# Projections in steps of one matmul pair, packed head rows and cropped convolution taps in a four-layer image kernel

## The reference, cut to what matters

```python
def _L0_conv_ref(x, w_qkv, w_proj, b_proj):       # layer 0: attention over 1024 pixels, 8 heads of 48 channels
    qkv = jnp.einsum('oc,bchw->bohw', w_qkv, x)
    att = softmax(einsum('bhxd,bhyd->bhxy', q * scale, k))
    out = jnp.einsum('bhxy,bhyd->bhxd', att, v)
    return jnp.einsum('oc,bchw->bohw', w_proj, out) + b_proj[None, :, None, None]

def deform_block(x, ow, ob, dw, pw, pb, K):       # layer 1: for K = 3, 5, 7, each on 128 channels
    offsets = conv2d(x, ow, ob, pad=K // 2)       # dense K x K convolution, 2 K K outputs, zero padding
    out = deform_depthwise(x, offsets, dw, K, K // 2)
    return conv2d(out, pw, pb, 0)
```

## Time and profile before

| | us |
|---|---|
| median of 3 runs (lowest, highest) | 6606.05 (6603.67, 6614.61) |
| the profiled execution | 6606.96 |
| its span | 6604.7 |
| PE busy | 5836.1 (88%) |
| DVE busy | 4831.0 (73%) |
| ACT busy | 3905.2 (59%) |
| POOL busy | 782.4 (12%) |

### The profile page before, as it was taken

The page is one execution under the profiler, slowest core; times in us unless marked ns, Lnnn a source line. Parts: engine busy times, 40 slices in busy tenths (PEclk is TensorE's granted clock), DMA queues, the critical chain, the costliest instruction groups (busy, mean ns, idle before and its releaser), DMA issues. The chain is left out here.

```text
span 6604.7 us, 121718 instructions
## 1 busy us (share of the span) xinstructions
PE 5836.1 (88%) x45996; PEld 3998.1 (61%) x45996; DVE 4831.0 (73%) x10089; ACT 3905.2 (59%) x5362; POOL 782.4 (12%) x780
## 2 busy tenths in 40 slices
PE   5999999999977888988989989899889899699798
PEld 2554454454434556875568855588655688455598
DVE  6887887787765778887788877798777888344433
ACT  3766776676652557875567855578755787112142
POOL 2222211222202002001011000110100100000000
PEclk9999999999998999999989999999999899899898
DMA  4111111112104445545445545455544454211598
GB/s 145 43 56 55 40 44 55 49 39 59 44 23 134 105 105 123 124 110 118 105 117 118 119 97 129 99 126 121 117 105 108 114 124 111 96 46 41 145 234 199
DMA packets 198408, 651.46 MB, mean 99 GB/s; under 512 B 61753, under 2 KB 68849, under 8 KB 154915
## 3 DMA queue, kind: packets, MB, share of 16 engines
q1 hardware_dynamic: 177747, 604.65, 37.2%
q0 software_dynamic: 19968, 37.78, 2.2%
HBM read 538.56 MB, written 65.59 MB: 91 GB/s over the span
## 5 line engine op out<-in xcount | busy, mean ns | idle before, releaser
L2367 PE MATMUL b_p<-b_work,b_hkt 64*128 64x144 f32 (+37 forms) x27520 | 2116.5, 309 | 253.1 <-DVE b_acc L2238 149.7
L2367 PEld LDWEIGHTS b_p<-b_work,b_hkt 64*128 64x128 f32 x27520 | 1966.0, 195 | 479.9 <-DVE b_work L2313 283.2
L2313 DVE TENSOR_TENSOR b_work<-b_work 128x140 f32<-128x140 f32 (+26 forms) x5312 | 1605.5, 353 | 228.6 <-PE b_p L2367 174.7
L2208 ACT ACTIVATE b_work<-b_work,b_mcol 128x512 f32<-128x512 f32 (+6 forms) x1328 | 764.9, 647 | 1021.4 <-DVE b_work L2313 883.3
L530 ACT ACTIVATE a_ex<-a_p_t 128x1024 f32<-128x1024 f32 x512 | 523.9, 1023 | 427.3 <-PE a_p_t L466 424.5
L2212 ACT ACTIVATE b_work<-b_work,b_mrow 128x544 f32<-128x544 f32 (+6 forms) x1328 | 762.2, 645 | 0.0
L2238 DVE SCALAR_TENSOR_TENSOR b_acc<-b_p,b_dwc,b_acc 128x323 f32<-128x323 f32 (+14 forms) x1088 | 621.6, 574 | 184.5 <-PE b_p L2367 184.5
L596 DVE TENSOR_REDUCE a_nm<-a_p_x 128x1 f16<-128x1024 f32 x512 | 624.3, 1219 | 154.0 <-PE a_p_x L455 145.8
L1779 PE MATMUL b_p<-b_hp,b_ow 128*98 128x512 f32 x1568 | 721.4, 611 | 0.0
L602 DVE TENSOR_TENSOR a_el<-a_ex,a_eh 128x1024 f16<-128x1024 f32 x512 | 682.1, 1332 | 7.0 <-ACT a_eh L535 6.9
L535 ACT CAST a_eh<-a_ex 128x1024 f16<-128x1024 f32 x512 | 535.4, 1046 | 54.8 <-ACT a_ex L530 3.8
(11 more groups left out here) (224 smaller groups left out, 5811.6 us busy)
## 6 DMA issues: line engine op xcount, KB each, us to landing
b_work<-sampling_positions SPq DMA_DIRECT2D x666, 512.0 KB, 6.5
d_win<-merged_kernels SPq DMA_DIRECT2D x192, 263.0 KB, 6.7
b_xin<-x SPq DMA_DIRECT2D x24, 1024.0 KB, 9.8
a_xr<-in_x SPq DMA_DIRECT2D x12, 1536.0 KB, 10.2
x<-a_xr SPq DMA_DIRECT2D x9, 1536.0 KB, 6.1
b_xr<-x SPq DMA_DIRECT2D x13, 1024.0 KB, 18.2
x<-b_xr SPq DMA_DIRECT2D x13, 1024.0 KB, 4.6
a_xh<-in_x SPq DMA_DIRECT2D x8, 1536.0 KB, 8.6
```

The costliest lines, as they stand in the source:

```text
L2208: last = e.activation(rx[:, u, xo[c]:xo[c + 1]].rearrange("p (a b) -> p a b", a=H), pp[:, b, 1, :].rearrange("p (a b) -> p a b", a=H)[:, : ...
L2313: e.tensor_tensor(S[:, k % NS, 0:(r1 - r0) * w].rearrange("p (a b) -> p a b", b=w), rx[:, u, xo[cc]:xo[cc + 1]].rearrange("p (a b) -> p a ...
L2367: last = e.matmul(G[:, a0 - top:z0 - top, c0 - left:c1 - left], hkt[64 * s:64 * s + 64, SIDE * cr + cc, :], S[64 * s:64 * s + 64, k % NS, ...
```

## The change

In layer 0 a query or key unit takes three slots with one matmul in each, so that nearly every slot carries one fp32 matmul; `UNIT_AT` and `OUT_AT` list the slot of each part. The loop now runs from slot 26 to 89. The output projection is three matmuls per tile over 128 packed rows: the head product is made by DVE into `o` (five slots after the head's last weighing slot, where POOL's was), and POOL then copies it by DMA into `packed`, in which the 384 head rows fill three blocks of 128. The add of bias and residual comes one slot after the tile's last matmul, the last tile's at the start of `statistics`. `norm` moves to slot 86 (22 of the next image), one image earlier than its projections need it; SP's loads and stores of whole images move to other heads. In layer 1 each tap of the offset convolutions reads and writes only the rectangle that lies in the image, and the middle tap comes first. The diff, cut to its core:

```diff
-    FIRST = 14
-    BEGIN = -36
+    FIRST = 26
+    BEGIN = FIRST - STEPS
     QUERY, KEY, VALUE = range(3)
     UNIT = ([(s, 0, n) for s in (QUERY, KEY) for n in range(2)] + [(VALUE, 0, c) for c in range(4)]
             + [(s, 1, n) for s in (QUERY, KEY) for n in range(2)] + [(s, 2, n) for s in (QUERY, KEY) for n in range(2)]
             + [(VALUE, 1, c) for c in range(4)])
-    UNIT_AT = (28, 31, 34, 37, 40, 43, 45, 47, 50, 53, 56, 59, 62, 65, 78, 80, 82, 84, 86, 88)
+    UNIT_AT = ([tuple(range(m, m + 3)) for m in range(26, 38, 3)] + [(m, m + 1) for m in range(38, 46, 2)]
+               + [tuple(range(m, m + 3)) for m in range(46, 70, 3)] + [(70, 71), (72, 73), (74, 74), (82, 82)])
     UNITS = len(UNIT)
-    OUT_AT = (71, 72, 73, 75, 76, 77)
-    NORM_AT = 26
+    OUT_AT = ((75, 76, 77), (78, 78, 79), (80, 80, 81), (83, 83, 84), (85, 86, 87), (88, 88, 89))
+    NORM_AT = 86
...
+    PACK = [[(j, *piece[1:]) for j in range(G3) for piece in PIECES[j] if piece[0] == hd] for hd in range(HEADS)]
+    PACKED = [16 * sum(len(PACK[hd]) for hd in range(p, HEADS, 2)) for p in range(2)]
...
-        wp = a.sb("wp", [TP, PAIRS, C])
+        wp = a.sb("wp", [P, G3, C])
...
-        o = a.sb("o", [TP, PAIRS, N])
+        o = a.sb("o", [TP, N])
+        packed = a.sb("packed", [P, G3, N])
...
-                for g in ((0,), (1, 2))[part]:
-                    last = e.matmul(p_j[:], wqk[:, g, s, j * P:(j + 1) * P], h[:, g, n * HALF:(n + 1) * HALF], start=(g == 0), stop=(g == G3 - 1))
+                last = e.matmul(p_j[:], wqk[:, part, s, j * P:(j + 1) * P], h[:, part, n * HALF:(n + 1) * HALF], start=(part == 0), stop=(part == G3 - 1))
...
-            if part == 1:
+            if part == len(UNIT_AT[unit]) - 1:
...
-        def unit_at(m, end):
-
-            for ahead in range(0, 1 if end else 2):
-                for unit, r in enumerate(UNIT_AT):
-                    if m - r + STEPS * (1 - ahead) in (0, 1):
-                        return ahead, unit, m - r + STEPS * (1 - ahead)
-            return None
+        def parts_at(m, end):
+
+            return [(ahead, unit, part) for ahead in range(0, 1 if end else 2) for unit, ms in enumerate(UNIT_AT)
+                    for part, at_m in enumerate(ms) if m == at_m - STEPS * (1 - ahead)]
+
+        def done_at(m, end):
+
+            return [(ahead, unit) for ahead, unit, part in parts_at(m, end) if part == len(UNIT_AT[unit]) - 1]
+
+        def outs_at(m):
+
+            return [(i, part) for i, ms in enumerate(OUT_AT) for part, at_m in enumerate(ms) if m == at_m]
...
-                    if not end:
-                        e.wait_ge(s_h.sem, s_h.at(b + 1))
-                        e.sem_inc(sh["tick"], 1)
-                        e.dma_start(xh[:].unsqueeze(1), xv[:, ds(b + 1, 1), :, :]).then_inc(s_xh.sem, 16)
...
-                        if hh == 0:
+                        if hh == 3:
                             e.wait_ge(s_st.sem, s_st.at(b))
                             e.sem_inc(sh["tick"], 1)
                             e.dma_start(yv[:, ds((b + B - 1) % B, 1), :, :], xr[:].unsqueeze(1)).then_inc(s_y.sem, 16)
-                        if hh == 1:
+                        if hh == 4:
                             e.wait_ge(s_y.sem, s_y.at((b + 1) * 16))
                             e.sem_inc(sh["tick"], 1)
                             e.dma_start(xr[:].unsqueeze(1), xv[:, ds(b, 1), :, :]).then_inc(s_xr.sem, 16)
+                        if hh == 1:
+                            if not end:
+                                e.wait_ge(s_h.sem, s_h.at(b + 2))
+                                e.sem_inc(sh["tick"], 1)
+                                e.dma_start(xh[:].unsqueeze(1), xv[:, ds((b + 2) % B, 1), :, :]).then_inc(s_xh.sem, 16)
...
-                        if hh % HEADS in (1, 2):
-                            e.wait_ge(s_fo.sem, s_fo.at(b * (2 * G3) + hh // HEADS * (2 * G3) + hh % HEADS * G3))
+                        if hh % HEADS in (2, 3):
+                            e.wait_ge(s_fo.sem, s_fo.at((b + hh // HEADS) * (2 * G3) + (hh % HEADS - 1) * G3))
...
-                    if unit_at(m, end):
-                        ahead, unit, part = unit_at(m, end)
+                    for ahead, unit, part in parts_at(m, end):
                         project(e, b + ahead, unit, part)
-                    if m in OUT_AT:
-                        i = OUT_AT.index(m)
+                    for i, part in outs_at(m) if m >= FIRST else ():
                         g, n = i // 2, i % 2
-                        if i == 0:
-                            e.wait_ge(s_n.sem, s_n.at((b + 1) * HEADS))
-                        else:
+                        if i == 0 and part == 0:
+                            for p in range(2):
+                                e.wait_ge(s_packed[p].sem, s_packed[p].at((b + 1) * PACKED[p]))
+                        elif part == 0:
                             e.wait_ge(s_fo.sem, s_fo.at(b * (2 * G3) + 2 * G3 + i))
-                        if i == 3 and not end:
-                            e.wait_ge(s_on.sem, s_on.at((b + 1) * (2 * HEADS) + 2))
-                        for t in range(PAIRS):
-                            last = e.matmul(p_o[2 if i < 3 else 0][:], wp[:, t, g * P:(g + 1) * P],
-                                            o[:, t, n * HALF:(n + 1) * HALF], start=(t == 0), stop=(t == PAIRS - 1))
-                        last.then_inc(s_f.sem, 1)
+                        if i % 3 == 0 and part == 0 and not end:
+                            e.wait_ge(s_on.sem, s_on.at((b + 1) * (2 * HEADS) + 2 + 2 * (i // 3)))
+                        last = e.matmul(p_o[0 if i < 3 else 2][:], wp[:, part, g * P:(g + 1) * P],
+                                        packed[:, part, n * HALF:(n + 1) * HALF], start=(part == 0), stop=(part == G3 - 1))
+                        if part == G3 - 1:
+                            last.then_inc(s_f.sem, 1)
...
-                    done = unit_at(m - 3, end)
-                    if done and done[2] == 1 and UNIT[done[1]][0] != VALUE and UNIT[done[1]][2] == 1:
-                        move(e, b + done[0], *UNIT[done[1]][0:2])
-                    k = m - 5 - BEHIND
+                    for ahead, unit in done_at(m - 3, end):
+                        if UNIT[unit][0] != VALUE and UNIT[unit][2] == 1:
+                            move(e, b + ahead, *UNIT[unit][0:2])
+                    k = m - 6 - BEHIND
                     if ends_head(k, end):
                         hh = k // NT
-                        r = ROWS_OF[hh % 2]
-                        e.wait_ge(s_d4.sem, s_d4.at((b * HEADS + hh + 1) * 16))
-                        e.wait_ge(s_on.sem, s_on.at(b * (2 * HEADS) + 2 * hh + 2))
-                        if hh % HEADS == 0:
+                        e.wait_ge(s_n.sem, s_n.at(b * HEADS + hh + 1))
+                        if hh % HEADS < 2:
                             e.wait_ge(s_f.sem, s_f.at((b + hh // HEADS) * (2 * G3)))
                         e.sem_inc(sh["tick"], 1)
-                        e.tensor_tensor(o[r:r + D, hh // 2 % PAIRS, :], osum[r:r + D, :, :].rearrange("p n q -> p (n q)"), denb[r:r + D, :], ALU.mult).then_inc(s_n.sem, 1)
+                        for j, d0, d1, r in PACK[hh % HEADS]:
+                            e.dma_start(packed[r:r + d1 - d0, j, :], o[ROWS_OF[hh % 2] + d0:ROWS_OF[hh % 2] + d1, :]).then_inc(s_packed[hh % 2].sem, 16)
...
+                def write_out(b, i):
+                    g, n = i // 2, i % 2
+                    if i == 0:
+                        e.wait_ge(s_xr.sem, s_xr.at((b + 2) * 16))
+                    e.wait_ge(s_f.sem, s_f.at(b * (2 * G3) + i + 1))
+                    part = xr[:, g, n * HALF:(n + 1) * HALF]
+                    e.scalar_tensor_tensor(part, p_o[0 if i < 3 else 2][:], bp[:, g:g + 1], part, ALU.add, ALU.add).then_inc(s_fo.sem, 1)
...
-                        e.wait_ge(s_n.sem, s_n.at(at(b, HEADS, hh - 1)))
...
+                    for i, part in outs_at(m - 1) if m > FIRST else ():
+                        if part == G3 - 1:
+                            write_out(b, i)
...
-                        norm(e, b + 1)
-                    done = unit_at(m - 2, end)
-                    if done and done[2] == 1:
-                        low(e, b + done[0], done[1])
+                        norm(e, b + 2)
+                    if m == NORM_AT - STEPS:
+                        norm(e, 1)
+                    for ahead, unit in done_at(m - 2, end):
+                        low(e, b + ahead, unit)
...
-                    if m in OUT_AT:
-                        i = OUT_AT.index(m)
-                        g, n = i // 2, i % 2
-                        if i == 0:
-                            e.wait_ge(s_xr.sem, s_xr.at((b + 2) * 16))
-                        e.wait_ge(s_f.sem, s_f.at(b * (2 * G3) + i + 1))
-                        part = xr[:, g, n * HALF:(n + 1) * HALF]
```

(29 more changed lines are left out.)

33 lines of the change are left out of this document (16 added, 17 removed).

## The result

The changed kernel takes 6438.05 us (median of 4 runs, 6433.8 to 6440.8) against 6604.86 us for the kernel before on the same chip: a ratio of 0.9744 (0.9727 to 0.9761), 167 us less. The forecast was 6405 us, 202 less than the profiled execution before, with a range of 6360 to 6490. The time is inside the range and 33 us above the forecast.

A forecast was written before the change was run, and what follows sets the result against it. In layer 0 it took DVE to bound bare steps and PE those with a projection; in layer 1's K = 5 stage DVE waited for PE. 6606.96 - 130 (layer 0) - 72 (layer 1) = 6405 us, range 6360 to 6490.

The forecast's parts named there:

- Its main term: Layer 1, K = 5 stage: cropped K = 7 taps save PE 13.7 us, of which 85% shortens the stage.
- the key move: Layer 0, move of key block 1: ACT blocks about 3.9 us and PE 2.7 per image.
- About 0.2 us at each of six heads: Layer 0, head ends: PE waits for copies and DVE's first addition, 1.2 us per image in all.
- Norm at 0.4: Layer 0, slot 22: norm, 2.4 us of DVE, no longer at a head's end, stalls 0.4 us instead of some 3.
- Statistics, forecast 5.2: Layer 0, before slot 26: last add, statistics, loop turn, additions and maximum delay the scores, stalling PE 5.2 us per image.
- Slot 18's wait: Layer 0: the next head's first weighing waits for DVE to free output tile 2's bank, 2.0 us per image.
- The edges: Layer 0's first image (-8), last image (-15), prologue (+5) and tail (-3): together -21 us.
- The product on VectorE: Layer 0: the head product takes DVE 1.13 us, 0.1 net without POOL's contention, costing nothing while PE is longer.
- A: Layer 0: DVE becomes the bound, an image takes 224 us and the layer saves 80; 6455 us, chance 0.18.
- B: Layer 1 gives nothing, as a shorter batch only makes PE wait for DVE later; 6477 us, chance 0.10.
- C: Layer 0: PE's half-rate clock stretches double, costing 28 us; 6433 us, chance 0.07.
- D: Layer 0: DVE waits for broadcast denominators, 3.6 us at each of 64 heads, 230 us in all; 6635 us, chance 0.04.

The follow-up runs named there:

- keys first: The changed kernel with keys projected before queries in the second and third row blocks: 6391.27 us, ratio 0.9677 against the kernel before.

## Why the prediction came out as it did

**Layer 1, right.** Forecast 72, measured 75 with the rectangles alone. Its main term, 85% of 13.7 us per K = 5 stage (11.6), came out at 11.6; the K = 3 stages gave 2.8 instead of 3.9, the K = 7 stages 3.2 instead of 1.5 (2.4 without the shorter cuts), the units ahead of the loop 3 instead of 4. In the K = 5 stage the batches are 4.97 to 6.06 us long but for one of 7.50 (4.9 to 6.0 forecast). VectorE's waits for PE in the K = 5 stage fell from 59.3 us to the 48 forecast:

```profile
DVE b_acc L2267 <- PE b_p L2396: 27.7, 16, 5.0
DVE b_work L2342 <- PE b_p L2396: 20.5, 9, 6.1
```

**Layer 0, mechanism right, sizes too small.** PE stayed the bound; bare steps became 3.03 and 3.15 us; the stalls came where they were forecast, and one more, and no rival took over. But layer 0 gave 82 us and not 130. The mis-sized terms:
- "ACT blocks about 3.9 us and PE 2.7" at the key move, and 1.7 for the clock behind it: ScalarE waits 4.9, PE 3.6, and the clock takes 2.4. That is 6.1 us per image where 4.4 was forecast. The order of keys and queries shows its price over the whole layer, 47 us. The forecast of the first image (8 us gained) left out that its move, ahead of slot 0, costs it that gain: it gained 0.6 us, and 6.9 with keys first.
- "About 0.2 us at each of six heads": 0.65 on average. I followed exponential, copies and first addition to the value products and left the maximum behind both additions out of the chain, though I counted it in slot 26.
- Norm at 0.4: I took slot 22 for free because no head ends there, and forgot that the head's product, new on VectorE, stands in it, five slots behind the head's last. Norm, product and maximum together hold slot 23 up by 1.7 us; without the product it is 0.35.
- The turn of the loop was counted on VectorE (0.9) and not on PE: 1.2 us in slot 25.
- Statistics, forecast 5.2 with VectorE's turn of the loop in it, were smaller: 3.2 us of wait in slot 26, or 4.4 with slot 25 just before it.
- Slot 18's wait was right (2.0). The clock took 4.6 us per image instead of 3.4: 2.4 in slot 63, 1.3 in slots 26 and 27, and 0.9 in slot 18, where the forecast had none.
- The edges, forecast -21, were -7: prologue +9.5, first image -0.6, last -12.4, tail -3.5.
- The six steady images gave 75 us, not 109. With 7 for 21 at the edges that is the 48 us by which layer 0 fell short. (One image of the kernel before took 240.9 us in its profile where the others took 231 to 234; in the two kernels that share its layer 0 the layer ended 6 and 9 us earlier, so the true gain may be nearer 75 than 82.)

Against these 48 us stood some 15 that I had not seen, in the K = 7 stages: 13 are the four cuts. That is why the time misses by 33 us only. This part is luck: the forecast was nearer than its first layer deserved.

**The product on VectorE.** Its size was right: it starts 1.14 us ahead of the next maximum (1.13 forecast), and with the contention gone (mean 1332 to 1214 ns for the subtraction, 60 us over the layer) it all but pays for itself: 64 products of 1.13 us are 72. By the total the moved product is worth nothing in time either way. It has a price in slot 23, beside norm, that the forecast left out; a product a slot away from norm was not tried.

```profile
876.70 1.21 DVE L641 TENSOR_TENSOR a_o<-a_osum,a_denb 48x1024 f32<-48x1024 f32 x1
877.84 1.21 DVE L614 TENSOR_REDUCE a_nm<-a_p_x 128x1 f16<-128x1024 f32 x1
```

**The rivals.** A (VectorE's pace): an image at 221.4 is near its 224, but 50 of 64 steps run at PE's own pace, so A is false as a bound; it holds for slots 18, 23 and 26 and for the head ends, where PE waits for VectorE. B: false. C: the clock stayed at 0.97 over the layer; behind the long waits it cost 4.6 us per image, 1.2 more than forecast. D: VectorE waited for denominators once, 4.6 us at the layer's end, and not at the other 63 heads.

## What to carry to other kernels

When work is spread evenly over the steps of the leading engine, the gain is what the stalls leave: go through every step that carries a second engine's extra piece, list all the pieces that fall in that step (norm and product fell in one here), and count that engine's whole chain up to each thing that the leader needs, not to the first. Then split what is found into waiting and working slowly: slot 63 looks like a stall of 2.4 us and has no wait in it. Of a wait on a buffer, ask how many transfers stand ahead of it in its queue; turning the order of keys and queries so that the shorter move is the last one waited for gave more (47 us) than any rearrangement of VectorE's work (0 to 13 us, not clear of noise). And measure a gain's place: 15 of the 167 us came in layer 1's K = 7 stages from an edit of layer 0.
